# Attention probabilities transposed by DMA instead of by TensorE, in an attention and feed-forward layer on eight cores

## Chip, cores and metric

One Trainium2 chip, eight cores, one launch. All eight cores run the same program on their own half of one of the four sequences: there is no traffic between cores. The metric is the device time in microseconds (us) of the slowest core. Engines are named as in the profile: PE is TensorE, DVE is VectorE, ACT is ScalarE, POOL is GpSimd, SP is SyncE.

## What is computed

```python
# x: (4, 4096, 1024) f32; 16 heads of 64, 2 key/value heads, window 256 (128 to each side)
q = (x @ Wq + bq); k = (x @ Wk + bk); v = (x @ Wv + bv)       # k, v: 2 heads, each for 8 query heads
scores = einsum('bgrsd,bgswd->bgrsw', qg, k_win)               # k_win: 256 keys around each row
probs = softmax(scores, axis=-1)
out = einsum('bgrsw,bgswd->bgrsd', probs, v_win) @ Wo + bo
x = layernorm(x + out)
# feed-forward
xr = mu_r*x + (1-mu_r)*x_prev;  xk = mu_k*x + (1-mu_k)*x_prev  # x_prev: the row before
x = layernorm(x + sigmoid(xr @ W_r.T) * (square(relu(xk @ W_k.T)) @ W_v.T))
```

## The kernel before

The kernel is written engine by engine. Each piece of work is a small function that is put on one engine's list with `sch.emit`; the lists are played out in exactly that order, and semaphores (the `Chan` objects) hold the engines apart. An engine that waits holds back everything behind it on its list. There are three stages, each a block of its own, so that a stage begins when all engines have ended the one before.

Stage A projects q, k and v. Stage B is attention with the output projection and the first layer norm. Stage C is the feed-forward layer.

The change is in stage B, and only there. Stage B goes over 17 row tiles `tau` of 128 rows. A tile has 16 heads, handled as 8 pairs `i`. For one tile:

- Scores (lines 466 to 491, PE). For a pair, each head first gets a mask matmul of 384 columns into a PSUM bank `psc` (L481), then q times k on top of it (L487). The bank `psc` has 3 slots, so that head H must wait for the exponential of head H-3 (channel `bEX`). Ahead of each pair stands a matmul of 512 columns (L479) whose result is overwritten at once by the mask matmul.
- Exponential (L499, ACT), which also sums each row into `sall`. After eight heads a reciprocal (L512, DVE) gives `rall`.
- Scaling (`fsc`, L525, DVE): `p16n[:, h]` = probabilities times reciprocal, bf16, 384 columns. `p16n` holds all 16 heads of one tile.
- Transposition (`ftm`, L542, PE): three 128x128 matmuls against the identity put the transposed probabilities of a head into `ppt` (2 slots of PSUM). `fpe` (L559, DVE) copies them to `pt16` in SBUF (4 slots, one for each head).
- Values (`fav2`, L574 and L579, PE): for a pair of heads six matmuls of 128 columns write the attention output into `po`; the two heads go to different halves of the array. Channel `bAV`.
- After pair 3 and pair 7, `fpo` (L596, DVE) copies `po` to `ao16`. Then `fwo` (L613, L617, PE) does the output projection: 16 matmuls of 512 columns and two for the bias.
- Layer norm (`ln`): `fz` (L628, DVE) adds the input rows `x32`, `fsq` (L635, ACT) squares and sums, `fvar` (DVE), `frst` (ACT) and `fy` (L677, DVE) finish it.

The rows of `x` that `fz` adds are loaded by `fx` (L461), one DMA of 512 KB for each tile, on SP's queue. It waits until `z` of two tiles earlier is done.

The order of the lists is a software pipeline, written out in lines 683 to 725. Iteration `tau` does the scores and exponentials of tile `tau`, and beside them scaling, transposition and values of tile `tau-1` (`emit_stage2`). On PE an iteration reads: scores of pair 0, scores of pair 1, stage 2 of pair 0, scores of pair 2, stage 2 of pair 1, and so on to stage 2 of pair 7, then the output projection of tile `tau-1`. The layer norm of tile `tau-2` is put on the DVE and ACT lists ahead of the scores of pair 3, so behind stage 2 of pair 1; the output projection that it reads ended just before the iteration began. After the 17th iteration stage 2, the projection and the layer norm of the last tile stand alone.

Of the kernel before, what the change touches and what calls it, by code (L numbers as in the profile page):

```python
# [7 lines left out]
F32 = mybir.dt.float32  # L8
BF16 = mybir.dt.bfloat16
# [13 lines left out]
HEADS = 16  # L23
WIN = 384
# [15 lines left out]
def wtok(e, *toks):  # L40
    for s, v in toks:
        if v > 0:
            e.wait_ge(s, v)
# [54 lines left out]
def build_nc(phases=3, astage=9):  # L98
    nc = bass.Bass("TRN2", target_bir_lowering=False)
# [56 lines left out]
    with (  # L156
# [19 lines left out]
        sch = Sched()  # L176
# [236 lines left out]
    with (  # L413
        nc.sbuf_tensor("p16", [128, 2, 16, WIN], BF16) as p16,
        nc.sbuf_tensor("p16n", [128, 16, WIN], BF16) as p16n,
        nc.sbuf_tensor("pt16", [128, 4, WIN], BF16) as pt16,
        nc.sbuf_tensor("ao16", [128, 2, 8, 128], BF16) as ao16,
        nc.sbuf_tensor("x32", [128, 2, D], F32) as x32,
        nc.sbuf_tensor("z32", [128, D], F32) as z32,
# [2 lines left out]
        nc.sbuf_tensor("rall", [128, 2, 16], F32) as rall,  # L422
        nc.sbuf_tensor("lnt", [128, 8], F32) as lnt,
        nc.psum_tensor("psc", [128, 3, 512], F32) as psc,
        nc.psum_tensor("ppt", [128, 2, 512], F32) as ppt,
        nc.psum_tensor("po", [128, 512], F32) as po,
        nc.psum_tensor("pwo", [128, 1024], F32) as pwo,
        ExitStack() as bst,
    ):
        bQK = Chan(nc, bst, "bQK")  # L430
        bEX = Chan(nc, bst, "bEX")
        bRC = Chan(nc, bst, "bRC")
        bSC = Chan(nc, bst, "bSC")
# [11 lines left out]

        sch = Sched()
        pt_toks = {}
        sch.emit("tensor", lambda e: wtok(e, v_maskq))
        sch.emit("scalar", lambda e: load_act_set(e, 6, nc))

# [2 lines left out]
        for tau in range(NTAU):  # L453
# [12 lines left out]
            for h in range(HEADS):  # L466
                H = 16 * tau + h
                g = h // 8
                ch = h % 8
                hb = 64 * g  # L470
                vqk = bQK.post()
                if h % 2 == 0:
                    def fmk2(e, tau=tau, H=H):
                        for dh in range(2):
                            HH = H + dh
                            if HH >= 3:
                                e.wait_ge(bEX.sem, HH - 2)
                            if dh == 0:
                                e.matmul(psc[:, HH % 3, 0:512], ident[:, :],  # L479
                                         k16[:, 0:512], start=True, stop=True)  # L480
                            e.matmul(psc[:, HH % 3, 0:WIN], ident[:, :], maskq[:, :],  # L481
                                     start=True, stop=False)
                    st_["qkpe"].append(fmk2)
                qb = 64 * (h % 2)
                ksrc = k16 if ((h % 2 == 0) == (g == 0)) else k16b
                def fqk(e, tau=tau, h=h, g=g, qb=qb, ksrc=ksrc, H=H):
                    e.matmul(psc[:, H % 3, 0:WIN],  # L487
                             qy[qb:qb + 64, tau, h // 2, :],
                             ksrc[qb:qb + 64, 1 + 128 * tau:1 + 128 * tau + WIN],
                             start=False, stop=True).then_inc(bQK.sem, 1)  # L490
# [26 lines left out]
            for h in range(HEADS):  # L517
                H = 16 * tau + h
                vsc = bSC.post()
                vrc_h = 2 * tau + h // 8 + 1  # L520
                def fsc(e, tau=tau, h=h, H=H, vrc=vrc_h):
                    e.wait_ge(bRC.sem, vrc)
                    if tau >= 1:
                        e.wait_ge(bTM.sem, 16 * (tau - 1) + h + 1)
                    e.tensor_scalar(p16n[:, h, :], p16[:, tau % 2, h, :],  # L525
                                    rall[:, tau % 2, h:h + 1], None, ALU.mult) \
                        .then_inc(bSC.sem, 1)
                st_["scale"].append(fsc)

            for h in range(HEADS):  # L530
                H = 16 * tau + h
                g = h // 8
                vsc_h = 16 * tau + h + 1
                vtm = bTM.post()
                war_tm = pt_toks.get(H - 2)
                def ftm(e, h=h, H=H, vsc=vsc_h, war=war_tm):
                    e.wait_ge(bSC.sem, vsc)
                    if war is not None:
                        wtok(e, war)
                    last = None  # L540
                    for c in range(3):
                        last = e.matmul(ppt[:, H % 2, c * 128:(c + 1) * 128],  # L542
                                        p16n[:, h, c * 128:(c + 1) * 128],
                                        ident[:, :], start=True, stop=True)
                    last.then_inc(bTM.sem, 1)
                st_["tpe"].append(ftm)
                eng = "vector"
                ech = bPE2V
                ech.post()
                pt_toks[H] = ech.tok()  # L550
                def fpe(e, H=H, vtm=vtm, eng=eng, ech=ech):
                    e.wait_ge(bTM.sem, vtm)
                    if H >= 4:
                        e.wait_ge(bAV.sem, H - 3)
                    if eng == "scalar":
                        e.copy(pt16[:, H % 4, :], ppt[:, H % 2, 0:WIN]) \
                            .then_inc(ech.sem, 1)
                    else:
                        e.tensor_copy(pt16[:, H % 4, :], ppt[:, H % 2, 0:WIN]) \  # L559
                            .then_inc(ech.sem, 1)  # L560
                st_["evac"].append((eng, fpe))
                vav = bAV.post()
                if h % 2 == 1:
                    tok_a = pt_toks[H - 1]
                    tok_b = pt_toks[H]
                    def fav2(e, tau=tau, h=h, g=g, H=H, tok_a=tok_a, tok_b=tok_b):
                        wtok(e, tok_a, tok_b)
                        if h % 8 == 1:
                            e.wait_ge(bPOE.sem, 2 * tau + (1 if h == 9 else 0))
                        slot = (h % 8) // 2  # L570
                        last = None
                        for c in range(3):
                            lhs = vt16[:, tau + c, 64 * g:64 * g + 64]
                            last = e.matmul(  # L574
                                po[0:64, slot * 128:(slot + 1) * 128], lhs,
                                pt16[:, (H - 1) % 4, c * 128:(c + 1) * 128],
                                start=(c == 0), stop=(c == 2),
                                tile_position=(0, 0), skip_group_check=True)
                            last = e.matmul(  # L579
                                po[64:128, slot * 128:(slot + 1) * 128], lhs,  # L580
                                pt16[:, H % 4, c * 128:(c + 1) * 128],
                                start=(c == 0), stop=(c == 2),
                                tile_position=(0, 64), skip_group_check=True)
                        last.then_inc(bAV.sem, 2)
                    st_["avpe"].append(fav2)
                else:
                    st_["avpe"].append(None)
                if h % 8 == 7:
                    half = h // 8
                    need_av = bAV.n  # L590
# [89 lines left out]

            sch.emit("sync", st_["fx"])
            pq = st_["qkpe"]

            def emit_stage2(src_st, i):
                sch.emit("vector", src_st["scale"][2 * i])
                sch.emit("vector", src_st["scale"][2 * i + 1])
                sch.emit("tensor", src_st["tpe"][2 * i])
                e0, f0 = src_st["evac"][2 * i]  # L690
                sch.emit(e0, f0)
                sch.emit("tensor", src_st["tpe"][2 * i + 1])
                e1, f1 = src_st["evac"][2 * i + 1]
                sch.emit(e1, f1)
                sch.emit("tensor", src_st["avpe"][2 * i + 1])
                for hh, fp in src_st["po"]:
                    if hh == 2 * i + 1:
                        sch.emit("vector", fp)
# [58 lines left out]
    with (  # L757
# [36 lines left out]
        sch = Sched()  # L794
# [329 lines left out]
```

## Time and profile before

| | |
|---|---|
| median of 3 runs | 1322.2 us (1318.06 to 1352.73) |
| the profiled execution's own time | 1318.19 us |
| its span on the slowest core | 1316.6 us (the eight cores: 1303.0 to 1316.6) |
| PE busy | 804.9 us, 61% |
| DVE busy | 486.1 us, 37% |
| ACT busy | 328.2 us, 25% |
| DMA of SP's queue (hardware_dynamic) | 17.32 MB, 3.9% of 16 engines |
| mean granted TensorE clock | 0.691 of full speed |

The span is the time from the first to the last instruction of a core. Busy shares are means over three stages with different limits. Stage B takes from about 220 us to about 934 us of the span, 54% of it.

### The profile page before, as it was taken

What the parts mean: (1) busy time and instruction counts of PE and PEld (TensorE: products, weight loads), DVE (VectorE), ACT (ScalarE), POOL (GpSimd) and SP (SyncE); (2) the same over time, 40 slices, a digit from 0 to 9 for tenths busy, and PEclk for the clock granted to TensorE, in tenths of its full rate; (3) what the DMA queues carried; (4) which work ended last, traced back from release to release, by engine and by line L of the source; (5) the groups of instructions that cost most, each with busy time, mean ns of one, the idle gap of its engine ahead of it and who ended that gap; (6) DMA issues with size and microseconds to landing.
All of it is one profiled execution on the core that took longest, in us unless ns stands there. A gap on an engine that the chain in (4) does not pass through costs nothing. (4 is left out here: it accounts for less than half of the span.)

```text
span 1316.6 us, 16258 instructions; the slowest of 8 cores (1303.0 to 1316.6 us)
## 1 busy us (share of the span) xinstructions
PE 804.9 (61%) x4114; PEld 351.6 (27%) x4189; DVE 486.1 (37%) x1241; ACT 328.2 (25%) x949; POOL 12.5 (1%) x20
## 2 busy tenths in 40 slices
PE   0588887666766666566665666654449259169093
PEld 0233333322222222222222222222114024024041
DVE  0223222333344333433334333344351632622714
ACT  0122223322223222232222322230113123123132
POOL 2000000000000000000000000000000000000000
PEclk9978877666656665576655666556559659669597
DMA  9845501000000000000000000000000100100101
GB/s 130 129 73 93 97 0 33 1 17 17 1 17 17 17 17 1 17 17 17 16 1 17 17 16 7 11 17 1 0 1 1 64 1 1 64 0 17 48 0 64
DMA packets 16085, 35.39 MB, mean 27 GB/s; under 512 B 3840, under 2 KB 3968, under 8 KB 16000
## 3 DMA queue, kind: packets, MB, share of 16 engines
q0 software_dynamic: 10384, 17.04, 8.2%
q1 hardware_dynamic: 5616, 17.32, 3.9%
q8 instruction: 41, 0.67, 0.2%
q14 instruction: 44, 0.36, 0.1%
HBM read 43.01 MB, written 8.39 MB: 39 GB/s over the span
## 5 line engine op out<-in xcount | busy, mean ns | idle before, releaser
L559 DVE CAST pt<-ppt 128x384 bf16<-128x384 f32 x272 | 139.2, 553 | 345.6 <-PE ppt L542 345.4
L499 ACT ACTIVATE p<-psc,konst 128x384 bf16<-128x384 f32 x272 | 155.3, 576 | 433.5 <-PE psc L487 433.0
L574 PE MATMUL po<-pt,vt 128*64 128x128 bf16 x408 | 64.2, 291 | 147.8 <-DVE pt L559 147.8
L542 PE MATMUL ppt<-ident,p16n 128*128 128x128 bf16 x816 | 103.4, 292 | 64.7 <-DVE p16n L525 64.7
L481 PE MATMUL psc<-maskq,ident 128*128 128x384 bf16 x272 | 99.6, 446 | 22.4 <-ACT p L499 11.8
L613 PE MATMUL pwo<-w16o,ao 128*128 128x512 bf16 x255 | 94.2, 519 | 26.5 <-DVE ao L596 23.1
L542 PEld LDWEIGHTS ppt<-ident,p16n 128*128 128x128 bf16 x816 | 70.2, 128 | 102.0 <-issue 101.7
L574 PEld LDWEIGHTS po<-pt,vt 128*64 128x64 bf16 x408 | 37.1, 143 | 177.8 <-issue 177.8
L895 PE MATMUL pr<-w16r,xr 128*128 128x512 bf16 x248 | 61.1, 408 | 33.5 <-DVE xk L874 31.8
L265 PE MATMUL paT<-ident,x16t 128*128 128x128 bf16 x224 | 47.8, 246 | 53.4 <-DMA x16t<-xpad 44.4
L525 DVE TENSOR_SCALAR p16n<-p,rall 128x384 bf16<-128x384 bf16 x272 | 72.3, 308 | 0.0
L373 PE MATMUL paP<-xfm,w16q 128*128 128x512 bf16 (+1 forms) x316 | 68.0, 380 | 1.7 <-issue 1.2
L579 PE MATMUL po<-pt,vt 128*64 128x128 bf16 x408 | 68.2, 301 | 0.0
L958 PE MATMUL pr<-w16vf,kact 128*128 128x512 bf16 x252 | 56.3, 379 | 12.4 <-DVE kact L939 6.7
L487 PE MATMUL psc<-k,qy 64*128 64x384 bf16 x136 | 59.2, 435 | 0.0
L487 PE MATMUL psc<-k16b,qy 64*128 64x384 bf16 x136 | 59.1, 435 | 0.0
L814 PE MATMUL pyf<-ident,qy 128*128 128x128 bf16 x24 | 5.0, 257 | 83.2 <-DVE yfm L823 82.8
L920 PE MATMUL pk<-xk,w16kf 128*128 128x512 bf16 x252 | 55.7, 379 | 0.2
L939 DVE TENSOR_TENSOR kact<-krelu 128x512 bf16<-128x512 bf16 x32 | 13.6, 425 | 108.5 <-ACT krelu L931 108.5
L499 ACT ACTIVATION_READ_ACCUMULATOR p<-psc,konst 128x1 f32 x272 | 53.4, 196 | 0.0
L284 DVE CAST xfm<-paT 128x128 bf16<-128x128 f32 x112 | 24.8, 284 | 75.9 <-PE paT L265 75.8
L479 PE MATMUL psc<-k,ident 128*128 128x512 bf16 x103 | 52.0, 505 | 0.0
(87 smaller groups left out, 820.0 us busy)
## 6 DMA issues: line engine op xcount, KB each, us to landing
x<-xpad SPq DMA_DIRECT2D x17, 512.0 KB, 3.6
out<-out SPq DMA_DIRECT2D x16, 512.0 KB, 2.6
x16t<-xpad POOLq DMA_DIRECT2D x5, 1024.0 KB, 11.0
w16q<-wq POOLq DMA_DIRECT2D x1, 2048.0 KB, 32.5
w16o<-wo POOLq DMA_DIRECT2D x1, 2048.0 KB, 53.6
w16r<-wr POOLq DMA_DIRECT2D x1, 2048.0 KB, 21.0
w16kf<-wkf POOLq DMA_DIRECT2D x1, 2048.0 KB, 21.1
w16vf<-wvf POOLq DMA_DIRECT2D x1, 2048.0 KB, 19.0
```

The costliest lines, as they stand in the source:

```text
L373: last = e.matmul(paP[:, par, 0:ncols], w16q[:, kc, dc * 128:(dc + 1) * 128], xfm[:, kc, 129:129 + ncols], start=(kc == 0), stop=(kc == NC ...
L481: e.matmul(psc[:, HH % 3, 0:WIN], ident[:, :], maskq[:, :], start=True, stop=False)
L487: e.matmul(psc[:, H % 3, 0:WIN], qy[qb:qb + 64, tau, h // 2, :], ksrc[qb:qb + 64, 1 + 128 * tau:1 + 128 * tau + WIN], start=False, stop=Tr ...
L499: e.activation(p16[:, tau % 2, h, :], psc[:, H % 3, 0:WIN], AF.Exp, bias=konst[:, 0:1], accum_out=sall[:, h:h + 1]).then_inc(bEX.sem, 1)
L525: e.tensor_scalar(p16n[:, h, :], p16[:, tau % 2, h, :], rall[:, tau % 2, h:h + 1], None, ALU.mult) \
L542: last = e.matmul(ppt[:, H % 2, c * 128:(c + 1) * 128], p16n[:, h, c * 128:(c + 1) * 128], ident[:, :], start=True, stop=True)
L559: e.tensor_copy(pt16[:, H % 4, :], ppt[:, H % 2, 0:WIN]) \
L574: last = e.matmul(po[0:64, slot * 128:(slot + 1) * 128], lhs, pt16[:, (H - 1) % 4, c * 128:(c + 1) * 128], start=(c == 0), stop=(c == 2), ...
L579: last = e.matmul(po[64:128, slot * 128:(slot + 1) * 128], lhs, pt16[:, H % 4, c * 128:(c + 1) * 128], start=(c == 0), stop=(c == 2), tile ...
L613: e.matmul(pwo[:, nh * 512:(nh + 1) * 512], ao16[:, tau % 2, kc, :], w16o[:, kc, nh * 512:(nh + 1) * 512], start=(kc == 0), stop=False)
L895: last = e.matmul(pr[:, pru % 2, nh * 512:(nh + 1) * 512], xr16[:, kc, ts * 128:(ts + 1) * 128], w16r[:, kc, nh * 512:(nh + 1) * 512], sta ...
L958: last = e.matmul(pr[:, pru % 2, nh * 512:(nh + 1) * 512], kact16[:, kc, ts * 128:(ts + 1) * 128], w16vf[:, kc, nh * 512:(nh + 1) * 512], ...
```

## The change

The transposition moves from PE to DMA. One DMA with `transpose=True` on SP's queue takes a pair of heads, reads `p16n` (128 partitions by 6 blocks of 128 columns) and writes `pt16` transposed block by block, 192 KB. There are 8 for each tile and 136 in all. They use four channels in turn (`trs`), so that up to four can be in flight. `pt16` grows from 4 to 8 slots, one for each head, so four pairs; a DMA waits until the value matmuls four pairs earlier have read its slots. The transposing matmuls, their PSUM tile `ppt` and the DVE copies are gone. Also gone are the 512-column matmuls of L479. The load of `x32` moves from SP's queue to POOL's.

```diff
@@ -413,7 +413,7 @@
-        nc.sbuf_tensor("pt16", [128, 4, WIN], BF16) as pt16,
+        nc.sbuf_tensor("pt16", [128, 8, WIN], BF16) as pt16,
@@ -422,12 +422,12 @@
-        nc.psum_tensor("ppt", [128, 2, 512], F32) as ppt,
+        trs = [Chan(nc, bst, "bTR%d" % i) for i in range(4)]
@@ -475,9 +476,6 @@
-                            if dh == 0:
-                                e.matmul(psc[:, HH % 3, 0:512], ident[:, :],
-                                         k16[:, 0:512], start=True, stop=True)
@@ -518,73 +516,64 @@
-                    if tau >= 1:
-                        e.wait_ge(bTM.sem, 16 * (tau - 1) + h + 1)
+                    if war is not None:
+                        wtok(e, war)                       # transpose DMA of this pair, tile before
...
+                def ftr(e, tau=tau, p=p, slot_a=slot_a, slot_b=slot_b, trc=trc,
+                        vtr=vtr, war_av=war_av):
+                    e.wait_ge(trc.sem, vtr - 16)
+                    e.wait_ge(bSC.sem, 16 * tau + 2 * p + 2)
+                    if war_av > 0:
+                        e.wait_ge(bAV.sem, war_av)
+                    e.dma_start(
+                        pt16[:, slot_a:slot_a + 2, :].rearrange(
+                            "p a (c b) -> p (a c) b", b=128),
+                        p16n[:, 2 * p:2 * p + 2, :].rearrange(
+                            "p a (c b) -> p (a c) b", b=128),
+                        transpose=True).then_inc(trc.sem, 16)
-                    for c in range(3):
-                        last = e.matmul(ppt[:, H % 2, c * 128:(c + 1) * 128],
-                                        p16n[:, h, c * 128:(c + 1) * 128],
-                                        ident[:, :], start=True, stop=True)
-                        e.tensor_copy(pt16[:, H % 4, :], ppt[:, H % 2, 0:WIN]) \
-                            .then_inc(ech.sem, 1)
...
                 def fav2(...):
-                        wtok(e, tok_a, tok_b)
+                    wtok(e, tok_tr)
@@ -680,19 +669,14 @@
-            sch.emit("sync", st_["fx"])
+            sch.emit("gpsimd", st_["fx"])
...
             def emit_stage2(src_st, i):
                 sch.emit("vector", src_st["scale"][2 * i])
                 sch.emit("vector", src_st["scale"][2 * i + 1])
-                sch.emit("tensor", src_st["tpe"][2 * i])
-                e0, f0 = src_st["evac"][2 * i]
-                sch.emit(e0, f0)
-                sch.emit("tensor", src_st["tpe"][2 * i + 1])
-                e1, f1 = src_st["evac"][2 * i + 1]
-                sch.emit(e1, f1)
-                sch.emit("tensor", src_st["avpe"][2 * i + 1])
+                sch.emit("sync", src_st["tpe"][i])
+                sch.emit("tensor", src_st["avpe"][i])
```

## Rows read from the trace of the kernel before

**Rows 1.** Busy time by window, 270.6 to 895.4 us: PE, PEld, DVE, ACT, POOL, granted clock, DMA.
```profile
270.60:895.40 624.80, 395.85 (x2266) 171.35 (x2310) 241.40 (x647) 172.71 (x540) 0.00 (x0) 0.61 0.05 14
```

**Rows 2.** Groups by line of one iteration, 564 to 605.1 us: busy, mean ns | idle before.
```profile
L559 DVE CAST pt<-ppt 128x384 bf16<-128x384 f32 x16 | 8.2, 553 | 20.9 <-PE ppt L542 20.9
```

**Rows 3.** Timeline of PE, same iteration: start us, us, instruction, idle before it and its releaser.
```profile
563.69 0.39 PE L479 MATMUL psc<-k,ident 128*128 128x512 bf16 x1
...
566.22 0.51 PE L542 MATMUL ppt<-ident,p16n 128*128 128x128 bf16 x6
568.01 0.22 PE L574 MATMUL po<-pt,vt 128*64 128x128 bf16 x1 [1.28 <-DVE pt L559]
...
576.48 0.80 PE L542 MATMUL ppt<-ident,p16n 128*128 128x128 bf16 x6 [4.30 <-DVE p16n L525]
578.30 0.28 PE L574 MATMUL po<-pt,vt 128*64 128x128 bf16 x1 [1.02 <-DVE pt L559]
...
582.22 0.28 PE L574 MATMUL po<-pt,vt 128*64 128x128 bf16 x1 [1.02 <-DVE pt L559]
...
582.68 0.61 PE L479 MATMUL psc<-k,ident 128*128 128x512 bf16 x1
583.08 0.85 PE L481 MATMUL psc<-maskq,ident 128*128 128x384 bf16 x2
...
584.30 0.82 PE L542 MATMUL ppt<-ident,p16n 128*128 128x128 bf16 x6
586.25 0.28 PE L574 MATMUL po<-pt,vt 128*64 128x128 bf16 x1 [1.13 <-DVE pt L559]
...
596.39 0.28 PE L574 MATMUL po<-pt,vt 128*64 128x128 bf16 x1 [1.02 <-DVE pt L559]
...
598.25 1.86 PE L613 MATMUL pwo<-w16o,ao 128*128 128x512 bf16 x4 [1.33 <-DVE ao L596]
...
604.77 0.39 PE L479 MATMUL psc<-k,ident 128*128 128x512 bf16 x1
```

**Rows 4.** Timelines of DVE and ACT in the same iteration.
```profile
570.67 1.22 DVE L628 SCALAR_TENSOR_TENSOR z<-pwo,x 128x1024 f32<-128x1024 f32 x1
...
575.91 0.54 DVE L525 TENSOR_SCALAR p16n<-p,rall 128x384 bf16<-128x384 bf16 x2
...
583.64 0.50 DVE L525 TENSOR_SCALAR p16n<-p,rall 128x384 bf16<-128x384 bf16 x2
...
569.49 0.58 ACT L499 ACTIVATE p<-psc,konst 128x384 bf16<-128x384 f32 x1 [1.77 <-PE psc L487]
...
571.99 1.06 ACT L635 ACTIVATE sqd<-z 128x1024 f32<-128x1024 f32 x1 [1.27 <-DVE z L628]
```

**Rows 5.** DMA issues: output and input, queue, count, KB each, median us from issue to landing.
```profile
x<-xpad SPq DMA_DIRECT2D x17, 512.0 KB, 3.6
...
w16k<-wk POOLq DMA_DIRECT2D x1, 256.0 KB, 16.1
w16v<-wv POOLq DMA_DIRECT2D x1, 256.0 KB, 19.2
...
bq_s<-bq SPq DMA_DIRECT2D x1, 4.0 KB, 1.6
```

**Rows 6.** Timeline of POOL at the start of the program: start us, us, instruction.
```profile
3.28 0.92 POOL L200 DMA_DIRECT2D w16k<-wk  x1
4.16 0.92 POOL L200 DMA_DIRECT2D w16v<-wv  x1
```

**Rows 7.** Timeline of PE: the first instruction after the first and after the 16th projection.
```profile
270.61 0.39 PE L479 MATMUL psc<-k,ident 128*128 128x512 bf16 x1
...
895.40 0.51 PE L542 MATMUL ppt<-ident,p16n 128*128 128x128 bf16 x6
```

**Rows 8.** Timeline of PE in the last tile's lone stage 2 and projection.
```profile
903.49 0.28 PE L574 MATMUL po<-pt,vt 128*64 128x128 bf16 x1 [1.02 <-DVE pt L559]
...
910.60 0.80 PE L542 MATMUL ppt<-ident,p16n 128*128 128x128 bf16 x6 [6.59 <-DVE p16n L525]
...
921.69 3.19 PE L613 MATMUL pwo<-w16o,ao 128*128 128x512 bf16 x7 [1.71 <-DVE ao L596]
```

More of the change, by code:

```diff
@@ L447, in build_nc @@
         pt_toks = {}
+        tr_toks = {}
         sch.emit("tensor", lambda e: wtok(e, v_maskq))
@@ L520, in build_nc, with fsc @@
                 vrc_h = 2 * tau + h // 8 + 1
-                def fsc(e, tau=tau, h=h, H=H, vrc=vrc_h):
+                war_tr = tr_toks.get((tau - 1, h // 2))
+                def fsc(e, tau=tau, h=h, H=H, vrc=vrc_h, war=war_tr):
                     e.wait_ge(bRC.sem, vrc)
-                    if tau >= 1:
-                        e.wait_ge(bTM.sem, 16 * (tau - 1) + h + 1)
+                    if war is not None:
+                        wtok(e, war)
                     e.tensor_scalar(p16n[:, h, :], p16[:, tau % 2, h, :],
@@ L528, in build_nc, with fav2 @@
                 st_["scale"].append(fsc)
-            for h in range(HEADS):
+            for h in range(1, HEADS, 2):
                 H = 16 * tau + h
                 g = h // 8
[L533 to L539, printed above, removed]
+                p = h // 2
+                gp = 8 * tau + p
+                trc = trs[gp % 4]
+                slot_a = (2 * p) % 8
+                slot_b = (2 * p + 1) % 8
+                war_av = 16 * tau + 2 * (p - 4) + 2 if p >= 4 else \
+                    (16 * (tau - 1) + 2 * (p + 4) + 2 if tau >= 1 else 0)
+                vtr = trc.post(16)
+                def ftr(e, tau=tau, p=p, slot_a=slot_a, slot_b=slot_b, trc=trc,
[10 more added lines that the diff above has]
+                        transpose=True).then_inc(trc.sem, 16)
+                st_["tpe"].append(ftr)
+                tok_tr = trc.tok()
+                tr_toks[(tau, p)] = tok_tr
+                vav = bAV.post(2)
+                def fav2(e, tau=tau, h=h, g=g, H=H, p=p, tok_tr=tok_tr,
+                         slot_a=slot_a, slot_b=slot_b):
+                    wtok(e, tok_tr)
+                    if h % 8 == 1:
+                        e.wait_ge(bPOE.sem, 2 * tau + (1 if h == 9 else 0))
+                    slot = (h % 8) // 2
@@ L540, in ftm @@
                     last = None
                     for c in range(3):
-                        last = e.matmul(ppt[:, H % 2, c * 128:(c + 1) * 128],
-                                        p16n[:, h, c * 128:(c + 1) * 128],
-                                        ident[:, :], start=True, stop=True)
[L545 to L556, printed above, removed]
-                            .then_inc(ech.sem, 1)
-                    else:
-                        e.tensor_copy(pt16[:, H % 4, :], ppt[:, H % 2, 0:WIN]) \
-                            .then_inc(ech.sem, 1)
@@ L561, in build_nc @@
[L561 to L566, printed above, removed]
-                        wtok(e, tok_a, tok_b)
[L568 to L571, printed above, removed]
-                        for c in range(3):
[L573 to L587, printed above, removed]
@@ new lines, in fav2 @@
+                        lhs = vt16[:, tau + c, 64 * g:64 * g + 64]
+                        last = e.matmul(
+                            po[0:64, slot * 128:(slot + 1) * 128], lhs,
+                            pt16[:, slot_a, c * 128:(c + 1) * 128],
+                            start=(c == 0), stop=(c == 2),
+                            tile_position=(0, 0), skip_group_check=True)
+                        last = e.matmul(
+                            po[64:128, slot * 128:(slot + 1) * 128], lhs,
+                            pt16[:, slot_b, c * 128:(c + 1) * 128],
+                            start=(c == 0), stop=(c == 2),
+                            tile_position=(0, 64), skip_group_check=True)
@@ L588, in build_nc @@
+                    last.then_inc(bAV.sem, 2)
+                st_["avpe"].append(fav2)
                 if h % 8 == 7:
```

## The prediction, made before the changed kernel ran

> **What bounds the kernel now.** I read the windows by stage first: the middle of stage B fills 624.8 us with PE busy 63% of it, DVE 39%, ACT 28%, at a granted clock of 0.61 [rows 1]. No engine is full, so order and waits set the time, not one engine's work. The timeline of PE shows which. From the first to the 16th projection's end there are 15 iterations in 895.40 - 270.61 = 624.8 us, 41.65 us each [rows 7]. I follow the one from 563.69 to 604.77 (41.08 us) and cut it at three points, writing AVn for the value matmuls of pair n [rows 3]:
>
> - projection end to AV2: 578.30 - 563.69 = 14.6 us;
> - AV2 to AV4: 586.25 - 578.30 = 7.95 us;
> - AV4 to the start of the projection: 598.25 - 586.25 = 12.0 us;
> - the projection: 604.77 - 598.25 = 6.5 us.
>
> In the cold part a pair costs PE 3.9 to 4.0 us. From AV3 to AV4 (582.22 to 586.25) it reads: values 0.46, the 512-column matmul 0.40, masks and scores 1.22, transposes 0.82, then a wait of 1.13 for DVE's copy. That wait stands ahead of AV in every pair, and scores of the next pair are behind it in PE's list, so ACT starves too. In the first segment there is one more wait, 4.30 us: pair 2's transposes wait for the scaling, which is behind the layer norm on DVE.
>
> **What the change removes.** Per iteration: 16 copies of 553 ns on DVE, 8.8 us [rows 2]; on PE, for each pair, the transposes (0.82), the wait (1.02 to 1.28) and the 512-column matmul (0.40): 2.3 us, 18 us over eight pairs. The cost of a cold pair falls to 0.46 + 1.22 = 1.68 us. ACT's two exponentials per pair take about 1.15 us, so PE keeps setting that pace.
>
> **What it adds.** In place of the wait for a copy PE waits for a DMA of 192 KB. Call L the time from the end of the second scaling to the start of AV, and s the time by which one transfer is behind the one before it. Where DVE can scale ahead, L is hidden; where it can't, L is paid whole. Walking the new lists:
>
> (1) Pairs 0 and 1. With no copies between them, DVE does four scalings right behind the last `po` copy, while PE runs the projection (6.5 us) and the first two score pairs (over 2 us). L is hidden up to 8 us. Cost nothing; the cover is the projection.
>
> (2) Pair 2. Its scaling stands behind the layer norm. Today z starts at 570.67, 7.0 us after the projection ended, because the copies of pairs 0 and 1 are ahead of it [rows 4]; it will start at once. But the square is behind six exponentials on ACT. The fifth starts today at 569.49, 5.8 us after the projection; pair 0's transposes and wait (566.22 to 568.01, 1.8 us) [rows 3] fall away, some of which the three slots of `psc` take back: I estimate 4.2 us. Two exponentials (1.15) on, the square starts at 5.4. From the square's start to the end of pair 2's scaling it is 576.45 - 571.99 = 4.5 us today [rows 4], unchanged. So AV2 starts at 9.9 + L, against 14.6.
>
> (3) Pair 3 was scaled with pair 2. AV2, scores, AV3: 1.68 us. Then `po` is copied and pair 4 scaled: 584.14 - 582.22 = 1.92 us after AV3's start [rows 3, 4], and with the hand-off 1.97. DVE couldn't go past `po`, so L is paid a second time: AV4 at 3.65 + L behind AV2, against 7.95.
>
> (4) Pairs 5, 6, 7 are scaled at once behind pair 4, 0.55 us apart. PE wants AV7 3.9 us after AV4 (scores and values of two pairs, then values alone, with the waits for `psc`). Then as today 598.25 - 596.39 = 1.86 us to the projection: 5.8 us, against 12.0, and max(0, 3s - 3.9) more.
>
> (5) The projection: 6.5 us, unchanged.
>
> Iteration: 25.85 + 2L + max(0, 3s - 3.9) + max(0, s - 1.7).
>
> **What a transposing DMA costs** no row shows. Below: SP's 4 KB load lands in 1.6 us and its 512 KB load in 3.6 us [rows 5]; between them 192 KB as a plain copy is 1.6 + 2.0 x 192/512 = 2.35 us, 0.75 of it transfer. The x rows are 4 KB long; here each piece is a block's row of 256 bytes. The nearest row with such pieces: w16k and w16v are written in 256-byte rows, 1024 of them each; they land at 3.28 + 16.1 = 19.4 and 4.16 + 19.2 = 23.4 us [rows 5, 6], so 4.0 us for 1024 rows, with other loads beside them and a cast. 768 rows are 3.0 us. So s lies between 0.75 and 3.0 if the bytes set it. I take 1.6, about their geometric mean and nearer to the quiet queue, since nothing else moves in stage B (DMA share 0.05 [rows 1]). For L I take 3.0 + s = 4.6: the 3.0 is x's 3.6 us less 0.8 for its bytes at the same slope, and 0.2 for the semaphores at both ends. A gain below a plain copy is excluded, since the bytes are the same.
>
> Two pages of the Trainium skill differ here. VectorE: DVE Perf Modes, The three transpose paths, gives the DMA crossbar 1309 ns for a 128x128 block against 390 ns for TensorE; six such blocks in a row would be an estimated s of 7.9 us. DMA: Bandwidth & Descriptors, Latency and other measured facts, gives an effective 261 GB/s, an estimated s of 0.75. By the formula above the one gives an iteration of some 74 us, the other some 33. No row here decides between them.
>
> **The sum.** Iteration: 25.85 + 9.2 + 0.9 = 35.95 us. Against 41.08 that is 5.1 us less; 15 iterations and the first one with a stage 2 make 16 x 5.1 = 82 us. The lone last tile: pairs 0 to 3 are scaled during the projection, so AV3 starts 1.4 us after 895.40 against 903.49; from AV3 to pair 4's scaling 7.1 us as today (910.60 - 903.49) [rows 8], then L + 3s + 1.86: the projection starts at 915.3 against 921.69, 6.4 us less. Together 88 us: 1318.2 - 88 = 1230 us. The profiled run is 4 us under the median of the runs, so the same sum is 1234 by the median.
>
> **Edits at no cost.** `x32` moves to POOL: its DMA starts as z of two tiles earlier ends and is wanted more than an iteration (36 us) later; were that cover gone it would cost some 4 us. Left on SP, it would have stood ahead of a tile's transposes waiting for z. The wait of the scaling for the DMA of the tile before is met long before. The slots' wait (four pairs back) is met too: AV of pair 4 waits `po` anyway.
>
> **Rivals.**
>
> (A) Short latency: the transfers cost no more than a plain copy, L 2.4 to 3.8, s 0.8. Iteration 30.7 to 33.5; 16 x 10.4 or 7.6, and 10 to 12 for the last tile: 1140 to 1186 us. For it: the idle DMA engines. Against it: pieces 16 times shorter than x's. 0.15.
>
> (B) Slower: the queue. Each transfer holds SP's queue or the DMA engines for s of 3 us or more. With L = 3.0 + s and both last terms open, the iteration is 25.85 + 6.0 + 2s + (3s - 3.9) + (s - 1.7) = 26.25 + 6s. It equals today's 41.1 at s = 2.5; from there the kernel is slower. At s = 3.0 it is 44.25, so 16 x 3.15 = 50 us more, 1368 us; at 4.0 it is 50.25 and the last tile 3 us longer, 1468 us. For it: the only measured row with short pieces gives 3.0, just past the point. Against it: that row was taken with the DMA engines full. Its far end: the six blocks of a transfer go one after another, each with the 1.6 us of a small load [rows 5], s = 9.6, iteration 84 us, about 2010 us. The crossbar figure above is the milder form of this, an estimated 1840 us. B 0.25 in all, 0.14 of it above 1460.
>
> (C) About even: s 2.2 to 2.8, the waits change their name and nothing else, 1288 to 1348 us. 0.12.
>
> (D) The clock. Without the transposes and the 512-column matmuls PE has longer pauses; if it stays at 1.2 GHz throughout, the projection (seven matmuls in 3.19 us when cold [rows 8]) takes 7.7 instead of 6.5 us and the first scores 0.8 more: 16 x 2 = 32 us on top, 1262 us. The clock is 0.61 today, so most of it is lost already. This lies inside the forecast's case.
>
> **How the numbers follow.** Forecast's case (s 0.8 to 2.2, with or without D): 1186 to 1290, 0.48; A 0.15; C 0.12; B 0.25. The likeliest is 1230. For 8 in 10 I leave out the lowest part of A (0.04) and B above 1460 (0.14): 1140 to 1460. Faster by over 2% (about what a measurement can tell from no change): 0.63; within 2%: 0.12; slower: 0.25.
>
> **What would show it.** Right: PE waits for a DMA ahead of AV2 and AV4 and hardly elsewhere; projections 36 us apart; z right behind the projection; from issue to landing of a transposing DMA about 4.4 us. B: waits ahead of AV5, 6 and 7 too, and issues on SP or landings spaced by 3 us or more. A: projections 31 to 33 us apart. D: clock 0.50 in the projection. What makes it wrong is s and L above all: each us in L is 2 us per iteration, 32 in the whole; each us in s past 1.7 is 6 per iteration.

## The result and the profile after

The changed kernel takes 1163.9 us (median of 8 runs, 1161.8 to 1166.7) against 1320.8 us for the kernel before in the same rounds: ratio 0.881, 95% interval 0.878 to 0.884, 12% faster. 1230 us was forecast. The profiled execution's span is 1167.2 us.

Busy time by stage, the kernel before: start and end, us, then PE, PEld, DVE, ACT, POOL, granted clock, DMA share, GB/s. The rows are stages A, B and C.

```profile
0.00:221.20 221.20, 148.50 (x634) 65.56 (x645) 53.19 (x156) 40.68 (x153) 12.48 (x20) 0.85 0.50 78
221.20:934.40 713.20, 447.09 (x2569) 193.65 (x2618) 273.85 (x733) 196.79 (x613) 0.00 (x0) 0.61 0.04 13
934.40:1316.60 382.20, 209.25 (x912) 92.37 (x928) 159.04 (x352) 90.70 (x184) 0.00 (x0) 0.75 0.06 23
```

The same of the changed kernel, with the 15 iterations between the first and the 16th projection's end as the last row, which answers [rows 1].

```profile
0.00:225.50 225.50, 148.77 (x635) 65.41 (x645) 53.17 (x156) 40.56 (x153) 12.46 (x20) 0.85 0.49 76
225.50:782.10 556.60, 311.20 (x1649) 108.88 (x1666) 136.65 (x461) 195.44 (x613) 9.01 (x17) 0.63 0.32 65
782.10:1167.20 385.10, 211.13 (x912) 93.20 (x928) 159.01 (x352) 90.78 (x184) 0.00 (x0) 0.74 0.06 22
268.10:752.40 484.30, 271.37 (x1455) 95.59 (x1468) 121.47 (x411) 171.17 (x540) 7.92 (x15) 0.64 0.32 67
```

The whole gain lies in stage B: 713.2 - 556.6 = 157 us. An iteration takes 484.3 / 15 = 32.3 us instead of 41.65. ACT's work is what it was. DVE lost 137 us of work and PE 136 us, but the granted clock hardly moved (0.61 to 0.63).

The timeline of PE in one iteration of the changed kernel; L479 is now the mask matmul, L565 the first value matmul of a pair, L602 and L606 the projection. It answers [rows 3].

```profile
527.32 0.50 PE L479 MATMUL psc<-maskq,ident 128*128 128x384 bf16 x2
...
529.63 0.24 PE L565 MATMUL po<-pt,vt 128*64 128x128 bf16 x1
...
540.12 0.29 PE L565 MATMUL po<-pt,vt 128*64 128x128 bf16 x1 [7.20 <-DMA pt<-p16n]
...
541.77 0.32 PE L565 MATMUL po<-pt,vt 128*64 128x128 bf16 x1
...
546.80 0.29 PE L565 MATMUL po<-pt,vt 128*64 128x128 bf16 x1 [3.03 <-DMA pt<-p16n]
...
551.77 0.28 PE L565 MATMUL po<-pt,vt 128*64 128x128 bf16 x1 [0.58 <-DMA pt<-p16n]
...
554.01 2.80 PE L602 MATMUL pwo<-w16o,ao 128*128 128x512 bf16 x7 [1.71 <-DVE ao L585]
...
559.21 0.50 PE L479 MATMUL psc<-maskq,ident 128*128 128x384 bf16 x2
```

AV0 starts 2.3 us after the projection and waits for nothing. The waits stand where the walk had put them: ahead of AV2, ahead of AV4, and a small one ahead of AV7.

One row misleads. On this core the record of each projection's first matmul is missing (255 matmuls of L602 are recorded where there are 272). The weight loads (PEld) are all there, and the first one shows that the projection starts at 553.6 and not at 554.01:

```profile
553.60 0.14 PEld L602 LDWEIGHTS pwo<-w16o,ao 128*128 128x128 bf16 x2 [1.54 <-issue]
```

The timelines of ACT (L624 is the layer norm's square), DVE (L524 is the scaling) and SP in the same iteration answer [rows 4]:

```profile
532.64 1.05 ACT L624 ACTIVATE sqd<-z 128x1024 f32<-128x1024 f32 x1
...
536.56 1.00 DVE L524 TENSOR_SCALAR p16n<-p,rall 128x384 bf16<-128x384 bf16 x4
...
543.20 1.87 DVE L524 TENSOR_SCALAR p16n<-p,rall 128x384 bf16<-128x384 bf16 x8
...
537.23 1.21 SPq L546 DMA_TRANSPOSE pt<-p16n  x1
...
543.83 1.21 SPq L546 DMA_TRANSPOSE pt<-p16n  x1
...
546.97 2.63 SPq L546 DMA_TRANSPOSE pt<-p16n  x2
```

Pair 2's second scaling ends at 537.10, its DMA is issued at 537.23 and AV2 starts at 540.12: L is 3.0 us. SP is held 1.21 us by each issue and issues one every 1.4 us. The four of pairs 4 to 7 run from 543.83 to 549.60, so the last is issued at 548.39, 4.56 us behind the first. The DMA issue row, which answers [rows 5]:

```profile
pt<-p16n SPq DMA_TRANSPOSE x136, 2.7
```

### The profile page after: what moved, and what is told of

Same layout as the page of the kernel before. It is cut to its first block and busy times, and to the rows that moved or that the text cites. A ratio compares the mean times of both kernels' runs of the same rounds, so it can differ in the third digit from the quotient of the medians.

```text
span 1167.2 us, 13437 instructions; the slowest of 8 cores (1151.5 to 1167.2 us)
## 1 busy us (share of the span) xinstructions
PE 671.1 (57%) x3195; PEld 267.5 (23%) x3237; DVE 348.8 (30%) x969; ACT 326.8 (28%) x949; POOL 21.5 (2%) x37
## 3 DMA queue, kind: packets, MB, share of 16 engines
q1 hardware_dynamic: 111968, 35.16, 14.3%
## 5 line engine op out<-in xcount | busy, mean ns | idle before, releaser
L565 PE MATMUL po<-pt,vt 128*64 128x128 bf16 x408 | 63.7, 289 | 177.1 <-DMA pt<-p16n 177.0
L479 PE MATMUL psc<-maskq,ident 128*128 128x384 bf16 x272 | 107.2, 428 | 34.5 <-ACT p L497 29.4
L602 PE MATMUL pwo<-w16o,ao 128*128 128x512 bf16 x255 | 91.6, 521 | 28.8 <-DVE ao L585 28.8
L585 DVE CAST ao<-po 128x512 bf16<-128x512 f32 x34 | 23.5, 692 | 206.8 <-PE po L570 206.8
L565 PEld LDWEIGHTS po<-pt,vt 128*64 128x64 bf16 x408 | 36.0, 141 | 213.2 <-issue 213.1
L879 PE MATMUL pr<-w16r,xr 128*128 128x512 bf16 x248 | 64.2, 423 | 33.5 <-DVE xk L858 31.8
L524 DVE TENSOR_SCALAR p16n<-p,rall 128x384 bf16<-128x384 bf16 x272 | 65.3, 309 | 0.1
L570 PE MATMUL po<-pt,vt 128*64 128x128 bf16 x408 | 65.1, 292 | 0.0
L617 DVE SCALAR_TENSOR_TENSOR z<-pwo,x 128x1024 f32<-128x1024 f32 x17 | 20.8, 1224 | 98.8 <-PE pwo L606 98.8
L602 PEld LDWEIGHTS pwo<-w16o,ao 128*128 128x128 bf16 x272 | 30.7, 123 | 76.9 <-issue 68.6
L833 ACT CAST yfm<-pyf 128x128 bf16<-128x128 f32 x64 | 17.2, 269 | 100.1 <-PE pyf L817 100.1
```

Of the source, the lines that this page charges most:

```text
L479: e.matmul(psc[:, HH % 3, 0:WIN], ident[:, :], maskq[:, :], start=True, stop=False)
L524: e.tensor_scalar(p16n[:, h, :], p16[:, tau % 2, h, :], rall[:, tau % 2, h:h + 1], None, ALU.mult) \
L565: last = e.matmul(po[0:64, slot * 128:(slot + 1) * 128], lhs, pt16[:, slot_a, c * 128:(c + 1) * 128], start=(c == 0), stop=(c == 2), tile_ ...
L570: last = e.matmul(po[64:128, slot * 128:(slot + 1) * 128], lhs, pt16[:, slot_b, c * 128:(c + 1) * 128], start=(c == 0), stop=(c == 2), til ...
L602: e.matmul(pwo[:, nh * 512:(nh + 1) * 512], ao16[:, tau % 2, kc, :], w16o[:, kc, nh * 512:(nh + 1) * 512], start=(kc == 0), stop=False)
L879: last = e.matmul(pr[:, pru % 2, nh * 512:(nh + 1) * 512], xr16[:, kc, ts * 128:(ts + 1) * 128], w16r[:, kc, nh * 512:(nh + 1) * 512], sta ...
```

## The experiments

The table below shows the experiments beside the two kernels. The times are medians, the legs means over the 15 iterations (us after the projection's end), the last column the length of stage B in the profiled execution, all on its slowest core. For the changed kernel and sf_psc5_ln, where the projection's first matmul has no record, its start is put 0.4 us ahead of the first recorded one; on the cores where all are recorded it is 25.8 to 26.0 and 14.7 to 14.8.

| kernel | time | iteration | AV2 | AV4 | next projection starts | stage B |
|---|---|---|---|---|---|---|
| before | 1320.8 | 41.65 | 15.2 | 23.2 | 35.2 | 713 |
| changed | 1163.9 | 32.3 | 12.9 | 19.7 | 25.9 | 557 |
| fill_back | 1159.1 | 32.35 (31.4 to 31.6 on the other cores) | 13.1 | 20.4 | 26.7 | 557 (541 to 544 on the other cores) |
| before_nofill | 1288.6 | 39.6 | 14.8 | 22.2 | 33.3 | 681 |
| x_on_sp | 1231.4 | 36.6 | 17.2 | 24.1 | 30.1 | 622 |
| dma_twice | 1308.9 | 40.7 | 14.2 | 23.8 | 34.0 | 704 |
| dma_per_head | 1280.3 | 38.5 | 13.7 | 22.4 | 32.2 | 666 |
| dma_quad | 1195.7 | 34.2 | 14.3 | 22.6 | 28.3 | 585 |
| before_scale_first | 1303.4 | 40.3 | 14.1 | 22.0 | 34.0 | 694 |
| scale_first | 1024.8 | 23.9 | 5.5 | 11.6 | 17.7 | 420 |
| sf_psc5_ln | 973.8 | 20.7 | 3.5 | 9.3 | 14.7 | 367 |
| sf_psc5_po | 959.4 | 19.8 | 3.4 | 8.5 | 13.8 | 353 |

### Is it the 512-column matmuls? fill_back and before_nofill

fill_back puts them back into the changed kernel; before_nofill takes them out of the kernel before.

```diff
+                            if dh == 0:
+                                e.matmul(psc[:, HH % 3, 0:512], ident[:, :],
+                                         k16[:, 0:512], start=True, stop=True)
```

> The changed kernel with the 512-column matmuls ahead of each score pair put back; nothing else. Theory (the gain is the DMA path, and the removed matmuls were mostly in PE's waits by then): in the changed kernel PE waits for ACT ahead of the second mask in pairs 0 to 2 (0.46 to 0.75 us) and for the DMA ahead of AV4 (3.0) and AV7 (0.6 to 1.4), so only the one between AV2 and AV3 is on the path (0.40), and part of those of pairs 6 and 7: 0.4 to 1.0 us per iteration, 6 to 16 us, 1170 to 1180 us. Rival (a good part of the gain is these matmuls themselves): 8 x 0.40 = 3.2 us per iteration, 51 us, about 1215 us. A second rival (they hold the clock up): 1164 us or less.

> The kernel before with only the 512-column matmuls taken out; the transposition stays on PE. Theory: there they are on PE's path in every pair from 3 on (5 x 0.40) and partly in pairs 0 to 2 (0.23 each when the clock is fast), 2.0 to 2.6 us per iteration: 32 to 42 us less, 1279 to 1289 us, and with the whole change's 157 us the DMA path is the larger part. Rival (without them the clock falls and takes the gain back): 1310 us or more.

before_nofill: 1288.6 us, ratio 0.975 (0.973 to 0.978), 32 us less, 2.1 us per iteration, as expected. The mean granted clock of its cores is 0.686 to 0.693, that of the kernel before 0.690 to 0.697: the clock took next to nothing back.

fill_back: 1159.1 us, ratio 0.878 (0.875 to 0.880), where 1170 to 1180 was expected: 5 us less than the changed kernel, which the second rival had forecast. Its stage windows (A, B, C) on the slowest core, core 7:

```profile
0.00:214.50 214.50, 150.52 (x644) 65.55 (x645) 53.14 (x156) 40.55 (x153) 12.45 (x20) 0.84 0.51 80
214.50:771.90 557.40, 329.02 (x1804) 112.55 (x1804) 137.93 (x461) 195.45 (x613) 9.01 (x17) 0.71 0.31 65
771.90:1156.20 384.30, 212.65 (x928) 92.93 (x927) 158.97 (x352) 90.78 (x184) 0.00 (x0) 0.75 0.06 22
```

On this core stage B is 557.4 us against 556.6, and the 11 us by which the profiled span is shorter are in stage A (214.5 against 225.5), which neither edit touches and which lay between 214 and 226 us in all profiles. But core 7 is the exception. On the other seven cores of this execution stage B takes 541.0 to 543.7 us, where the eight cores of the changed kernel take 554.6 to 558.3. Stage B of core 0:

```profile
217.50:761.00 543.50, 308.34 (x1769) 109.81 (x1802) 138.19 (x461) 195.22 (x613) 9.06 (x17) 0.73 0.32 67
```

The mean over the eight cores is 1145 to 1149 us in the four executions of fill_back and 1156 to 1159 us in the nine of the changed kernel: 11 us less. The time of the slowest core shows only 5 of them. So in the changed kernel these matmuls cost nothing; they give back about 0.9 us per iteration on seven cores. Two things meet there. The next projection starts 0.7 to 0.8 us later (26.6 to 26.8 against 25.8 to 26.0), as the theory said. And the projection itself is shorter, as the second rival said: 4.7 to 5.0 us on seven cores and 5.6 on core 7, against 6.3 to 6.5 in the changed kernel. One iteration of fill_back on core 0, the part up to the projection and the projection, with its matmuls (L605 there):

```profile
605.74:632.17 26.43, 12.93 (x87) 4.59 (x89) 7.17 (x24) 11.40 (x36) 0.53 (x1) 0.74 0.30 65
632.17:636.46 4.29, 4.29 (x19) 1.57 (x19) 1.00 (x5) 0.00 (x0) 0.00 (x0) 1.00 0.47 91
...
632.17 1.89 PE L605 MATMUL pwo<-w16o,ao 128*128 128x512 bf16 x8 [1.34 <-DVE ao L588]
633.99 0.39 PE L609 MATMUL pwo<-bo,ones 1*128 1x512 bf16 x1
634.31 1.90 PE L605 MATMUL pwo<-w16o,ao 128*128 128x512 bf16 x8
```

The granted clock is 1.00 in this projection (2.4 GHz), 0.9 in the mean of the projections on these seven cores, 0.78 on core 7 and 0.65 to 0.68 in the changed kernel. Why core 7 got less of it is open. So the same matmuls cost 32 us on the kernel before and gain a little on the changed one. In the changed kernel PE is waiting anyway and the clock rises with them; in the kernel before the clock of stage B was 0.61 with them and 0.60 without.

### Does the place of the x load matter? x_on_sp

```diff
-            sch.emit("gpsimd", st_["fx"])
+            sch.emit("sync", st_["fx"])
```

> The changed kernel with the load of x32 back on SP's queue. It stands there ahead of a tile's eight transposes and waits for z of two tiles earlier, which ends 1.3 us after the projection. Theory: AV0 can't start before 1.3 + 0.1 + 0.33 + 3.0 = 4.7 us after the projection instead of 2.3, and the exponentials of pair 2 and the square behind them shift with it: 2.4 us per iteration, 38 us, about 1202 us. Rival (the wait is covered, the move to POOL is worth nothing): 1164 us.

1231.4 us, ratio 0.932 (0.929 to 0.934): 67 us more than the changed kernel, 4.3 us per iteration. The direction is the theory's, the size nearly twice its 2.4. SP and PE of one iteration; the projection ended at 377.02:

```profile
378.65 0.33 SPq L462 DMA_DIRECT2D x<-xpad  x1
379.17 2.29 SPq L546 DMA_TRANSPOSE pt<-p16n  x1
...
384.10 0.29 PE L565 MATMUL po<-pt,vt 128*64 128x128 bf16 x1 [4.70 <-DMA pt<-p16n]
```

SP waits for z, issues x at 378.65, and the first transpose at 379.17, 2.15 us after the projection. The theory had it at 1.73, so 0.4 us more are here. And AV0 comes 4.9 us behind this issue instead of 2.9 (in the mean of the 15 iterations 4.5). The other 1.5 us are this, because the transpose lands late: over the iterations the first one behind x lands 4.1 us after its issue in the median, the second 3.3, and those of the pairs after them 2.7 as ever. The load of x, issued just ahead, takes 3.9 us to land, so the two are in flight together. That the one slows the other is read from these figures; no run changed the size of the load. That this transpose holds SP for 2.29 us is the exception: in 14 of the 15 iterations it is 1.21 to 1.23. The Trainium skill (DMA: Bandwidth & Descriptors, Issuing engines are not separate DMA queues) says that DMAs of all issuing engines run on the same 16 engines and that spreading them only saves the issuing time. The trace doesn't contradict it. The move to POOL gains because POOL does the waiting for z, and because the transposes of pairs 0 and 1 are done before x starts: on its slowest core no transpose of the changed kernel was in flight together with a load of x. Where the two do meet on two queues, in sf_psc5_po below, the transpose is late as well.

### What does a transposing DMA cost, and is it on the path? dma_twice, dma_per_head, dma_quad

dma_twice issues each DMA twice, the first into a tile that nobody reads. dma_per_head takes 3 blocks per DMA in place of 6, dma_quad 12.

```diff
 # dma_twice
+                    e.wait_ge(txc.sem, vtx - 16)
+                    e.dma_start(ptx[:, slot_a:slot_a + 2, :]..., p16n[:, 2 * p:2 * p + 2, :]...,
+                        transpose=True).then_inc(txc.sem, 16)
 # dma_per_head
+                    for hd in range(2):
+                        e.dma_start(pt16[:, slot_a + hd, :]..., p16n[:, 2 * p + hd, :]...,
+                            transpose=True).then_inc(trc.sem, 16)
 # dma_quad, on even pairs only, behind four scalings
+                        pt16[:, slot_a:slot_a + 4, :]..., p16n[:, 2 * p:2 * p + 4, :]...
```

> The changed kernel with every transposing DMA issued twice, the first into a tile that nobody reads. The transpose then costs two issues on SP (1.4 us apart as measured) and two transfers. Theory (SP's issue spacing and the latency of a transfer both lie on the path, at the places of the prediction's walk): AV2 and AV4 each 1.4 us later, AV3 1.1 us later (2.8 behind AV2 instead of 1.7), AV7 8.4 us behind AV4 instead of 4.5 to 5: 7.8 us per iteration, with the last tile about 125 us, 1270 to 1300 us. Rival (only the DMA engines' 0.9 us of a transfer counts, and it is mostly hidden): less than 60 us more, 1225 us at most.

> The changed kernel with one transposing DMA for each head (3 blocks of 128x128) instead of one for each pair (6 blocks). Tells what SP's 1.21 us per issue are made of. Theory: they go by blocks, so an issue takes about 0.6 to 0.7 us, a pair 1.4 to 1.8, and the time is 1164 to 1195 us. Rival (a fixed cost of each transposing DMA): 1.2 us each, 2.8 per pair, and the time is that of the doubled DMA, 1270 us or more.

> The changed kernel with one transposing DMA for two pairs (12 blocks of 128x128), issued behind four scalings. From the runs so far an issue costs SP 1.2 us with 3 and with 6 blocks, and the landing is 2.3 and 2.7 us. Theory (the issue is a fixed cost, the transfer goes by blocks at 0.13 us each): issue 1.2, landing 3.5; AV2 and AV4 each 1.3 us later (0.5 for two more scalings, 0.8 for the landing), AV7 no longer behind four issues, 1.1 us earlier: 1.5 us per iteration, about 24 us, 1175 to 1200 us. Rival (above some size an issue is split and costs 2.4 us): 1210 us or more.

dma_twice: 1308.9 us, ratio 0.990 (0.988 to 0.993), 145 us more than the changed kernel; 125 was expected, less than 60 by the rival. An iteration is 8.4 us longer. That nearly undoes the change: of the 12% gained, 1% is left. dma_per_head: 1280.3 us, ratio 0.969 (0.964 to 0.973). My theory, that SP's time goes by blocks, fell. This run moves the same bytes in twice the issues and loses 116 of the 145 us, so most of the loss of dma_twice is the issues, not the bytes. dma_quad: 1195.7 us, ratio 0.906 (0.903 to 0.909), inside the expected 1175 to 1200.

The transposing DMAs of the changed kernel, then of dma_per_head, then of dma_quad: count, ns on SP's queue (least, median, greatest), and us from issue to landing.

```profile
L546 SPq DMA_TRANSPOSE pt<-p16n x136: 1209/1210/2533, 241.0 to 764.3; - x136
...
DMA to landing us min/median/max: 2.7/2.7/4.2
```

```profile
L547 SPq DMA_TRANSPOSE pt<-p16n x272: 1162/1214/2207, 240.3 to 873.0; - x136
...
DMA to landing us min/median/max: 2.3/2.3/4.2
```

```profile
L550 SPq DMA_TRANSPOSE pt<-p16n x68: 1275/1456/2567, 238.0 to 787.5; - x68
...
DMA to landing us min/median/max: 3.7/3.8/4.3
```

With 3, 6 and 12 blocks an issue holds SP for 1.2, 1.2 and 1.5 us: nearly a fixed cost, 3.7 times the 0.33 us of an ordinary DMA's issue. The landing is 2.3, 2.7 and 3.8 us: 0.13 to 0.18 us for each further block of 32 KB, 180 to 250 GB/s. One DMA for two pairs is slower all the same, since pair 2 then waits for pair 3's scaling and for the longer transfer. Six blocks is the best of the three sizes in this order of the lists.

### Are the two exposed latencies a matter of order? scale_first and before_scale_first

scale_first puts the 16 scalings of a tile at the head of its iteration on DVE's list. before_scale_first does the same with the kernel before.

```diff
+            if prev is not None:
+                for fs in prev["scale"]:
+                    sch.emit("vector", fs)
             def emit_stage2(src_st, i):
-                sch.emit("vector", src_st["scale"][2 * i])
-                sch.emit("vector", src_st["scale"][2 * i + 1])
```

> The changed kernel with all 16 scalings of a tile put at the head of its iteration on DVE's list, ahead of the layer norm and the first copy of po; nothing added or removed. Theory (the latency of the DMA, 3.0 us, is paid twice per iteration only because pair 2's scaling stands behind the layer norm and pair 4's behind the copy of po): both waits go, AV2's with the 4.5 us of the layer norm chain ahead of it. PE then goes at ACT's and psc's pace of 1.7 to 1.9 us a pair: projection 5.5, first two score pairs 2.3, seven more steps of 1.8 = 12.6, the layer norm's 2.5 us on ACT, 1.9 to the projection: about 25 us instead of 31.9, 16 x 7 = 110 us less, 1040 to 1090 us. Rival (the issue of a transposing DMA on SP, 1.4 us each, or the slots of pt16 set the pace): less than 40 us of it, 1125 us or more.

> The kernel before, transposing on PE, with only the order of scale_first: all 16 scalings of a tile at the head of its iteration. Theory (the DMA's worth is that it takes the copies off DVE's list; without it pair 2's copy still stands behind the layer norm and every pair still waits for its own copy): the scaling's 0.5 us goes from behind the layer norm, from ahead of z and from ahead of pair 4, and pair 2's transposes (0.6 us) run early: 1.2 to 2.2 us per iteration, 20 to 35 us, 1285 to 1300 us. Rival (the order alone brings most of what scale_first won): 1250 us or less.

scale_first: 1024.8 us, ratio 0.777 (0.775 to 0.778), 139 us less than the changed kernel; 110 was expected. before_scale_first: 1303.4 us, ratio 0.986 (0.984 to 0.988), 18 us less than before; 20 to 35 was expected. So the order alone is worth 18 us, the DMA alone 157, both 296. With the transposition on PE the scalings go ahead too, but the copy of each pair is still on DVE's list, behind the layer norm, and PE waits for every one of them. Between 300 and 800 us of before_scale_first (us in all, times, longest):

```profile
PE po L574 <- DVE pt L559: 137.4, 99, 4.5
```

In the same stretch the kernel before waits 104.2 us for the copies and 46.3 for the scaling; the second wait is gone here, and most of it has become the first. Only once DVE has nothing between scaling and `po` does the new order pay. PE in one iteration of scale_first, whose projection ended at 448.68; the waits ahead of the masks are most of what is left:

```profile
453.69 0.32 PE L479 MATMUL psc<-maskq,ident 128*128 128x384 bf16 x1 [0.46 <-ACT p L497]
...
454.21 0.24 PE L565 MATMUL po<-pt,vt 128*64 128x128 bf16 x1
...
457.48 0.48 PE L479 MATMUL psc<-maskq,ident 128*128 128x384 bf16 x1 [2.64 <-ACT p L497]
...
466.58 1.86 PE L602 MATMUL pwo<-w16o,ao 128*128 128x512 bf16 x4 [1.33 <-DVE ao L585]
```

### How far it goes: sf_psc5_ln and sf_psc5_po

The 2.64 us are ACT doing the layer norm while `psc` holds only one head ahead. sf_psc5_ln gives `psc` the two banks of `ppt` and moves Ln and Exp. sf_psc5_po also moves the rest of the layer norm behind pair 3's copy.

```diff
-        nc.psum_tensor("psc", [128, 3, 512], F32) as psc,
+        nc.psum_tensor("psc", [128, 5, 512], F32) as psc,
-                            if HH >= 3:
-                                e.wait_ge(bEX.sem, HH - 2)
+                            if HH >= 5:
+                                e.wait_ge(bEX.sem, HH - 4)
+                if i == 3 and prevprev is not None:   # sf_psc5_po: i == 4, between var and y
+                    sch.emit("scalar", prevprev["rst"])
```

> scale_first with two further edits: psc gets 5 slots in place of 3, in the two PSUM banks that ppt had, and the layer norm's Ln and Exp stand on ACT's list behind the exponentials of pair 3 instead of ahead of them. Theory: in scale_first a pair takes 1.93 us where PE's own work is 1.68, and between AV2 and AV3 4.1 us, 2.2 more, because ACT does the layer norm there and psc holds only one head ahead. With both gone an iteration of 24.0 us becomes 20.5 to 21.5 us, 40 to 55 us less than 1025: 970 to 985 us. Rival (the granted clock or ACT's own pace holds the pair at 1.9 us): more than 1005 us.

> sf_psc5_ln with the rest of the layer norm (variance, Ln and Exp, the normalised row) placed behind pair 3's copy of po on DVE's list and behind the exponentials of pair 4 on ACT's. In sf_psc5_ln PE waits 2.4 us ahead of AV4 for that copy, because it stands behind the layer norm; nothing waits for the layer norm soon. Theory: that wait goes down to 0.5 or less and PE's own work of 1.68 us a pair when cold is left: 1.5 to 2.2 us per iteration, 24 to 35 us less than 974: 938 to 950 us. Rival (PE meets ACT instead, whose 16 exponentials, square, Ln and Exp are 11.5 us busy in an iteration but come late): less than 12 us of it.

sf_psc5_ln: 973.8 us, ratio 0.736 (0.734 to 0.738), as expected. It makes two edits at once, and no run tells them apart. sf_psc5_po: 959.4 us, ratio 0.727 (0.725 to 0.729): 14 us less, where 24 to 35 was expected and under 12 was the rival's. The wait ahead of AV4 in sf_psc5_ln, and in its place the one in sf_psc5_po:

```profile
437.15 0.29 PE L565 MATMUL po<-pt,vt 128*64 128x128 bf16 x1 [2.38 <-DVE ao L585]
```

```profile
397.00 1.20 SPq L546 DMA_TRANSPOSE pt<-p16n  x1
...
397.26 0.53 POOL L462 DMA_DIRECT2D x<-xpad  x1 [19.89 <-DVE z L617]
...
403.86 0.29 PE L565 MATMUL po<-pt,vt 128*64 128x128 bf16 x1 [1.91 <-DMA pt<-p16n]
```

The wait for the copy is gone and one for the DMA stands in its place. Pair 4's transpose waits for AV0 (396.56) to free its slots and is issued at 397.00, and the load of x, which waits for z, at 397.26: both are then on the DMA engines. AV4 comes 6.9 us behind the issue, where 2.9 was the rule; the greatest landing of a transpose in this kernel is 7.3 us. The whole trace says the same: of the transposes issued with no other transpose in flight, the 9 that overlap a load of x land after 6.7 us in the median, the 17 that don't after 2.75; the loads of x themselves take 6.1 us instead of 3.9. In sf_psc5_ln the two medians are 6.1 (10 of them) and 2.8 (17). No run moved the load away, and more slots of `pt16` weren't tried either.

## Why the prediction was right, step by step

- **The number.** The forecast was 1230 us and 1163.9 was measured. That is not in the forecast's own case (1186 to 1290, chance 0.48) but in the range of rival A (1140 to 1186, chance 0.15): a short latency, 31 to 33 us per iteration. The walk through the lists was right and the DMA was priced too high. The stated 1140 to 1460 holds the result because it reaches far to both sides, not because the price was known.
- **What bounds the kernel.** Order and waits, not an engine's work: shown. scale_first removes no work at all and takes 139 us.
- **The removed 512-column matmuls.** The 18 us of PE's work and waits per iteration that the text listed were not all on the path, and the sum didn't use them so. Taking the 512-column matmuls out gains 2.1 us per iteration in the kernel before. In the changed kernel taking them out loses time: with them back, seven of eight cores are about 0.9 us faster per iteration. The prediction had no such term.
- **(1) Pairs 0 and 1 hidden.** Right: AV0 at 2.3 us, no wait.
- **(2) Pair 2.** The square was put at 5.4 us after the projection; it starts at 5.3 (532.64 - 527.32). From its start to the scaling's end 4.46 us, as before. AV2 at 9.9 + L: 12.9 us with the measured L of 3.0, and 12.9 is the mean.
- **(3) Pair 4.** 3.65 + L is 6.65; measured 6.68.
- **(4) The end of the pairs.** 5.8 + max(0, 3s - 3.9) gives 6.5 us with 3s = 4.56. Measured from AV4 to the projection's first weight load it is 6.8 here and 6.3 in the mean. The 0.4 us more of this iteration: pair 7 is used 3.4 us after its issue (551.77 - 548.39), not 3.0.
- **(5) The projection.** 6.5 us was taken; it is 6.4 in the mean and 5.6 in the iteration shown. Rival D (a colder clock) didn't come: 0.64 against 0.61.
- **The cost of a DMA** is the term that was mis-sized. L was 4.6 and is 3.0; s was 1.6 and is 1.4 to 1.5. The step that failed is the one that built L as 3.0 + s and filled s from the startup loads. The 3.0 has a slip in it: it takes 0.8 us off x's 3.6 "for its bytes", but by the slope used there x's 512 KB are 2.0 us (0.75 is the share of 192 KB). Done rightly it is 3.6 - 2.0 + 0.2 = 1.8, L is 3.4 with the same s, and the sum gives about 1190 us. The landing is 2.7 us from the start of the issue, within 0.4 us of the plain copy estimated at 2.35; 0.3 us are the hand-offs. Rival A had this latency. And s isn't set by short pieces on the DMA engines, as the text argued from the startup loads, but by SP's issue. L shorter by 1.6 us, twice per iteration and 15 times, is 48 us, most of the 66 by which the forecast was too high (1230 against 1164). The end of the pairs (6.3 us instead of 6.7) is another 6, the projection 2, and the last tile, which gained 9 instead of 6, is 3. The iteration before was taken as 41.08 us, the one walked, and is 41.65 in the mean: 8 us.
- **Rival B.** Its formula is 26.25 + 6s, so 6 us per iteration for each us in s. dma_twice doubles the issues, adding 1.4 us: 8.4 us, or 8.1 with the last term at nothing below s = 1.7; 8.4 are measured. Its turning point of 2.5 us is too low. At a spacing of 2.8 us the formula gives 43.05 us and dma_twice takes 40.7, still 1% faster than before, since L there is 4.4 us (14.2 - 9.9), not 3.0 + s. The far end, blocks one after another, is refuted: six blocks land in 2.7 us. The 1309 ns that the Trainium skill (VectorE: DVE Perf Modes, The three transpose paths) gives for one block would have made six of them an estimated 7.9 us. The trace doesn't agree with that reading of the figure.
- **The x load.** "At no cost" was right for POOL. What it would have cost on SP I had only named: 67 us, measured.

Open: why some issues take SP up to 2.5 us (the greatest of the row above), and why the third of four in a row starts 0.3 us late. Nothing was run to tell a full queue from busy DMA engines.

## What to carry over

Moving a step to another engine is worth most by what it takes off the lists of the engines that waited for it. Before such a move, walk the in-order lists and note at each point whether the new latency can be covered, then reorder so that its inputs are produced early: here the same DMA cost 6 us of latency per iteration in one order and next to nothing in the other (6.6 us of waits in the whole of scale_first, against 177.0). And an edit's value must be measured on the kernel that it goes into: the same matmuls cost 32 us on one and gained 5 on the next (11 in the mean of the cores). Look at all cores before calling two times equal: the slowest one of fill_back hid what seven others showed.

## What the runs showed of the hardware

- A transposing DMA holds SP for 1.2 us with 3 or 6 blocks of 128x128 bf16 and 1.5 us with 12, against 0.33 us for a plain one; it lands after 2.3, 2.7 and 3.8 us.
- Right behind a 512 KB load on the same queue, the same transpose landed 4.1 us after its issue in the median instead of 2.7 (x_on_sp); SP was held no longer, 1.2 us in 14 of 15.
- Beside a 512 KB load from POOL's queue a transpose landed after 6.7 us in the median and up to 7.3 (sf_psc5_po), where 2.7 was the least.
- With 8 more matmuls of 512 columns per iteration of the changed kernel the granted clock in stage B was 0.71 to 0.73 instead of 0.63 to 0.64. The projection took 4.7 to 5.0 us (seven cores) or 5.6 (one) instead of 6.3 to 6.5, and stage B 541 to 544 us on those seven instead of 555 to 558. In the kernel before, taking them out left the mean clock of the cores at 0.69.
